# One DVE operation for the bias of the attention's exponentials, in a fused adaLN, attention and mixture-of-experts kernel

## The reference, cut to what matters

```python
ctx_k = jnp.concatenate([sink_k, win_k], axis=2)       # 4 sinks, then a window of 128
logits = jnp.einsum('bhqd,bhkd->bhqk', q, ctx_k) * scale
logits = jnp.where(mask, logits, -jnp.inf)             # cols <= rows + (t_ctx - t)
w = jax.nn.softmax(logits, axis=-1)
w = jnp.where(jnp.isnan(w), jnp.zeros_like(w), w)
out = jnp.einsum('bhqk,bhkd->bhqd', w, ctx_v)
```

## Time and profile before

| | us |
|---|---|
| three runs | 356.20, 357.07, 358.56 |
| median | 357.07 |
| the profiled execution, its own time | 358.24 |
| its span, first to last instruction | 356.5 |
| what lies around the span | 1.74 |
| PE / DVE / ACT / POOL busy in the span | 284.6 / 236.4 / 163.0 / 203.9 |

### The profile page before, as it was taken

How to read it: one execution, slowest core, us unless ns; L and a number is a source line. 1 busy time by engine, 2 the same in 40 slices (tenths; PEclk the granted TensorE clock), 3 DMA queues, 4 the chain that set the end, 5 groups by cost and what they waited for, 6 DMA issues and landing times.

```text
span 356.5 us, 6304 instructions
## 1 busy us (share of the span) xinstructions
PE 284.6 (80%) x1665; PEld 219.3 (62%) x1666; DVE 236.4 (66%) x911; ACT 163.0 (46%) x518; POOL 203.9 (57%) x254
## 2 busy tenths in 40 slices
PE   4898889888989798989865899899979899986000
PEld 4364466656857485747634798789878787775000
DVE  0476477998789887997884654644443577753991
ACT  3142552267135733456212355455544566653550
POOL 3613107728674677558467265556645478773981
PEclk9996996999799996999886699999999999998655
DMA  7949001123615629702285543455546678857895
GB/s 271 310 135 340 3 2 59 62 72 122 192 49 160 178 88 324 182 30 76 75 223 189 199 143 112 149 150 163 157 129 197 190 238 252 259 170 243 305 332 182
DMA packets 41439, 59.81 MB, mean 168 GB/s; under 512 B 5092, under 2 KB 29880, under 8 KB 41404
## 3 DMA queue, kind: packets, MB, share of 16 engines
q1 hardware_dynamic: 34312, 39.91, 38.4%
q0 software_dynamic: 6528, 17.90, 13.9%
q10 hardware_dynamic: 564, 1.59, 1.2%
HBM read 33.57 MB, written 25.80 MB: 167 GB/s over the span
## 4 chain that ended last, share of the span: by engine, by line
PE 40%; DVE 28%; DMA 9%; issue 8%; another core or an unknown queue 5%; ACT 4%; POOL 2%; SPq 1%; DVEq 0%; POOLq 0%; ACTq 0%
PE bank L1225 13%; PE bank L1235 8%; PE bank L890 6%; PE bank L1083 4%; DMA p_win<-slots 3%; PE bank L1050 2%; DVE st L1338 2%; DVE h_sb L1364 2%; PE bank L1027 2%; DVE xs L1386 2%; DMA ht<-in_L_attn_x_dram 2%; PE bank L933 1%; DVE top_i L1381 1%; DVE act_sb L1376 1%
## 5 line engine op out<-in xcount | busy, mean ns | idle before, releaser
L646 POOL DMA_INDIRECT ys<-pt_win,row_i x72 | 71.2, 989 | 56.8 <-ACT pt_win L674 30.3
L1225 PE MATMUL bank<-ht,w_now 128*128 128x128 f32 x576 | 79.7, 283 | 5.4 <-DVE xs L1386 5.4
L593 POOL DMA_INDIRECT slots<-h_sb,slot_i x64 | 63.0, 984 | 32.8 <-DVE slot_i L1435 17.4
L1225 PEld LDWEIGHTS bank<-ht,w_now 128*128 128x128 f32 x576 | 73.4, 199 | 6.2 <-DVE xs L1386 5.6
L1733 DVE TENSOR_TENSOR act_t<-bank,sg 128x128 f32<-128x128 f32 x72 | 20.9, 290 | 52.2 <-ACT sg L841 37.0
L1235 PE MATMUL bank<-w_dn,act_t 128*128 x144 | 45.5, 399 | 6.5 <-DVE act_t L1733 4.9
L674 ACT ACTIVATE ht<-bank 128x256 f32<-128x256 f32 x104 | 39.9, 383 | 22.3 <-PE bank L890 17.6
L674 ACT ACTIVATE pt_win<-bank 128x256 f32<-128x256 f32 (+1 forms) x88 | 37.2, 423 | 23.5 <-PE bank L1235 13.0
L1083 PE MATMUL bank<-w_route,ht 128*128 128x272 f32 x128 | 41.3, 450 | 4.8 <-ACT ht L674 1.7
L890 PE MATMUL bank<-ident,p_win 128*128 128x128 f32 x198 | 36.6, 281 | 5.7 <-DMA p_win<-slots 3.8
L841 ACT ACTIVATE sg<-bank 128x128 f32<-128x128 f32 x72 | 20.1, 279 | 44.4 <-PE bank L1225 20.8
(11 more groups left out here) (260 smaller groups left out, 501.3 us busy)
## 6 DMA issues: line engine op xcount, KB each, us to landing
p_win<-slots SPq DMA_DIRECT2D x67, 129.0 KB
slots<-pads SPq DMA_DIRECT2D x28, 129.0 KB
xs<-in_L_attn_x_dram SPq DMA_DIRECT2D x3, 1024.0 KB
wmod_sb<-ys SPq DMA_DIRECT2D x12, 256.0 KB
w_gu<-ys SPq DMA_DIRECT2D x10, 256.0 KB, 2.9
mod_bc<-mod_rows_out SPq DMA_DIRECT2D x4, 512.0 KB, 5.9
w_dn<-in_L_ffn_w_down_dram SPq DMA_DIRECT2D x1, 2048.0 KB
h_sb<-ys SPq DMA_DIRECT2D x8, 256.0 KB
```

Of the source, the lines that this page charges most:

```text
L593: pool.indirect_dma_start(out=slots, out_offset=bass.IndirectOffsetOnAxis(ap=slot_i[:, k, j:j + 1], axis=0), in_=h_sb[:, j, :], in_offset= ...
L646: pool.indirect_dma_start(out=ys, out_offset=bass.IndirectOffsetOnAxis(ap=row_i[:, col:col + 1], axis=0), in_=y_sb[:, k, :], in_offset=Non ...
L1225: last = mm(bank[2 + k % 2][:, half * P:(half + 1) * P], w_now[:, k % 2, c, half * M:(half + 1) * M], ht[:, k, c, :], start=(c == 0), stop ...
```

## The change

The bias of a group becomes one operation on DVE behind the maximum: less_max = min(-SCALE * m_win, less_sink), where less_sink = -SCALE * m_sink is computed once per batch, right behind m_sink. The tile m_all goes. The sinks' exponent becomes SCALE * logit + less_max in one scalar_tensor_tensor, with the same bias as the window's, so ACT's exponential at L713 has no scale any more. Since that operation now reads less_max, it waits for at_sub of the last group first.

```diff
@@ at_exp (ACT)
-                    act.activation(p_sink[:], p_sink[:], ACT.Exp, scale=SCALE).then_inc(S["at_exp"], 1)
+                    act.activation(p_sink[:], p_sink[:], ACT.Exp).then_inc(S["at_exp"], 1)
@@ DVE
             def at_sink_max(b, at):
                 dve.wait_ge(S["at_log"], b * (HG + 1) + 1)
                 at.done(v.tensor_reduce(m_sink[:], ls, AX.X, ALU.max))
+                at.done(v.tensor_scalar(less_sink[:], m_sink[:], -SCALE, None, ALU.mult))
 
             def at_less_max(b, g, at):
 
                 dve.wait_ge(S["at_log"], b * (HG + 1) + g + 2)
                 hs = slice(4 * g, 4 * g + 4)
                 at.done(v.tensor_reduce(m_win[:, hs], lws[g], AX.X, ALU.max))
-                at.done(v.tensor_tensor(m_all[:, hs], m_win[:, hs], m_sink[:, hs], ALU.max))
-                v.tensor_scalar(less_max[:, hs], m_all[:, hs], -SCALE, None, ALU.mult).then_inc(S["at_sub"], 1)
+                v.scalar_tensor_tensor(less_max[:, hs], m_win[:, hs], -SCALE, less_sink[:, hs], ALU.mult, ALU.min)\
+                    .then_inc(S["at_sub"], 1)
 
             def at_sinks_less_max(b):
-                v.tensor_tensor(p_sink[:], ls, m_all[:].unsqueeze(2).to_broadcast([P, H, SINKS]), ALU.subtract)\
+                wait_apart(dve, S["at_sub"], b * (HG + 1) + HG)
+                v.scalar_tensor_tensor(p_sink[:], ls, SCALE, less_max[:].unsqueeze(2).to_broadcast([P, H, SINKS]),
+                                       ALU.mult, ALU.add)\
                     .then_inc(S["at_sub"], 1)
```

More of the change, by code:

```diff
@@ L175, in bass_adaln_attention_moe @@
         m_win = sb("m_win", [P, H])
-        m_all = sb("m_all", [P, H])
+        less_sink = sb("less_sink", [P, H])
         less_max = sb("less_max", [P, H])
```

## The result

The changed kernel takes 352.01 us (median of 4 runs, 351.41 to 353.70); the kernel before, beside it, 357.01 (4 runs, 356.20 to 358.56). The ratio is 0.9862 with a 95% interval of 0.9814 to 0.9911: 1.4% faster, 4.9 us. I had forecast 356.9 with a range down to 355.3.

What follows compares the result with a forecast made beforehand. The prediction took a chain of waits, PE 40% and DVE 28%, as the bound, with four of 16 groups on it. Its terms, -0.22 + 3 x 0.01 = -0.19 us, put on the median 357.07, gave 356.9 us, range 355.3 to 358.6.

Steps and rivals of the forecast that it cites:

- the price of the edited operations: Attention: removed m_all with its wait -0.22 us in batch 0, -0.19 in others; less_sink +0.20 in batches 1 to 3.
- rival B: Batches 2 and 3: POOL's multiplications hold less_sink, 0.58 for 0.17 us, +1.2 in three batches, 358.1 us; chance 0.1.
- the narrow escape that was forecast: Batch 2: less_sink just escapes POOL's pair of multiplications, which ends at 114.86; less_sink on its own at 114.93.
- the sum: Whole kernel: -0.22 us in batch 0 and +0.01 in each of batches 1 to 3, -0.19 together.
- idle time: DVE: busy time falls by 2 to 3 us of 236.4, and almost all of it becomes idle time.
- my -0.19 us: Whole kernel: the forecast's net change in time, likeliest ends -0.25 and +0.06 us.
- groups 1 to 3 of batches 1 to 3 give nothing: Batches 1 to 3: an earlier less_max there is of no use; group 3's saving runs into DVE's idle 0.71 us.
- rival A: Batches 1 to 3, group 3: less_max escapes POOL's L618, DVE 0.61 us earlier three times, 355.1 us; chance 0.07.
- rival C: Behind the last batch: a 6.01 us stretch ends by its own clock, earlier arrival is waited away, 357.1 us; chance 0.2.

Runs made afterwards that it cites:

- after_pad3: The changed kernel with 3 tiny memsets at the head of DVE's stream, against the kernel before: 356.64 us, ratio 0.9994.
- after_third: The changed kernel run again, without padding, beside the padded ones on one chip, against the kernel before: 353.72 us, ratio 0.9895.
- batches123_only: The change in batches 1 to 3 alone, batch 0 in the old form, against the kernel before: 356.73 us, ratio 1.0002.
- before_same: The kernel before, unedited, run once more as a control against itself: 357.06 us, ratio 1.0005.
- before_pad3: The kernel before with 3 tiny memsets at the head of DVE's stream, against the kernel before: 356.79 us, ratio 1.0017.

## Why the prediction was wrong

**Right: the price of the edited operations.** For batch 0 I had -0.22; all eight profiles with the change in batch 0 and in the others, padded or not, on four chips, have 3.79 or 3.80 from the logits of group 3 to down(0, 3) where the unchanged ones have 3.99 or 4.00, so -0.20, and a doubled m_all gives +0.19. By the rule of the Trainium skill ("VectorE: DVE Perf Modes", section "The DRAIN you can't avoid") that the semaphore costs nothing extra, it could have been 0.07; these profiles decide for the rows. The fused operation takes 0.164 (I took 0.17, ends 0.16 and 0.21), p_sink 0.206 for 0.204, less_sink 0.17 in batches 1 to 3 (0.35 in batch 0, where it is off the chain and costs nothing, as forecast). DVE's busy time fell by 4.3 us and not by 2 to 3: the two groups m_all and less_max had 7.9 us with those that POOL held, and less_max and less_sink have 3.5, with no less_max held. From m_sink to the logits of group 2 nothing changes, 3.37 in both.

**Right: rival B does not happen.** The timeline of batch 2 after the change:

```profile
111.70 1.59 POOL L599 TENSOR_TENSOR scaled<-scaled,mod_bc 128x256 f32<-128x256 f32 x2 [2.51 <-ACT scaled L733]
112.96 0.21 DVE L1307 TENSOR_REDUCE m_sink<-bank 128x16 f32<-128x64 f32 x1
113.21 0.17 DVE L1308 TENSOR_SCALAR less_sink<-m_sink 128x16 f32<-128x16 f32 x1
```

POOL ends at 113.29 and less_sink at 113.38, unheld, 0.09 behind: the narrow escape that was forecast (0.04).

**Wrong, the step that failed: the sum has no term for where DVE's later instructions stand in its stream, and takes what the change removes elsewhere to become "idle time".** The sum priced instructions by their durations and by what waits for them, and took everything behind the edited places as moving along unchanged. But removing instructions also moves all later ones to other places in DVE's stream. In batch 1 this alone is worth 0.69 us (32.01 to 31.32 between after_pad3 and after_third), more than three times what I had summed for the whole change: 0.32 of it the late start, and 0.30 to 0.31 a collision with POOL that it had brought about. Over the whole kernel, with everything equal but the place and the three operations, it is 353.72 against 356.64 us. How the 0.69 becomes 2.9 is not shown: the two profiled executions need the same 121.87 us for all the batches, since after_third gives 0.5 back in batch 2, and differ by 3.3 in the experts' stage, which is less than two traces of the kernel before differ by. Off chip B, three places of the changed kernel have 0.9895, 0.9994 and 0.9906, three of the kernel before 1, 1.0017 and 0.9938. With the old place at batch 1's head the change is worth 0.9994 [0.995, 1.0039], which holds the 0.9995 of my -0.19 us, but is too wide to confirm it.
The Trainium skill ("Runtime: NRT & Kernel Launch", section "Instruction fetch mechanics") says that an engine's instructions are refilled in blocks while it executes, and that the fetch is hidden behind the pace at which instructions are issued. By that rule a place in the stream costs next to nothing. The trace agrees on the blocks (packets of 8,192 and 16,384 bytes on two instruction queues); on the hiding it would disagree only if the gap is the fetch's, which is open.

**Not right as it stood: groups 1 to 3 of batches 1 to 3 give nothing.** The escape of rival A did come. The timeline of batch 1, group 3, which answers to the earlier trace rows:

```profile
84.07 0.16 DVE L1315 SCALAR_TENSOR_TENSOR less_max<-m_win,less_sink 128x4 f32<-128x4 f32 x1
84.11 0.74 POOL L618 TENSOR_TENSOR wsd_gated<-wsd_sb,mod_bc 128x256 f32<-128x256 f32 x1
84.15 0.28 DVE L1374 SCALAR_TENSOR_TENSOR act_sb<-sg,bank 128x128 f32<-128x128 f32 x1
...
84.95 0.67 PE L1103 MATMUL bank<-wsd_gated,act_t 128*128 128x256 f32 x2 [0.88 <-ACT act_t L674]
...
85.65 0.48 DVE L1367 SCALAR_TENSOR_TENSOR h_sb<-scaled,rstd,mod_bc 128x256 f32<-128x256 f32 x1 [0.40 <-issue]
```

less_max starts 0.04 us ahead of POOL's L618 and takes 0.16 instead of 0.58; the longest of all sixteen takes 0.18. PE gets nothing of it up to down(1, 3), as argued: that stretch is 6.74 after and 6.71 before. Behind it there is a difference that I had not considered. From down(1, 3) to the values of batch 1, nine traces with the old form in that batch have 3.30 three times and 3.48 to 3.70 six times; nine with the new form have 3.30 nine times. The late one is ACT's copy of group 3's probabilities: in before it idles 0.54 us,

```profile
89.27 0.60 ACT L674 ACTIVATE pt_win<-bank 128x512 f32<-128x512 f32 x1 [0.54 <-PE bank L890]
```

and in batches123_only 0.16:

```profile
89.22 0.60 ACT L675 ACTIVATE pt_win<-bank 128x512 f32<-128x512 f32 x1 [0.16 <-issue]
```

behind the same instructions of ACT and PE in the same order. What sets it free I do not know. A similar stretch of batch 2 is 3.30 or 3.82 in traces of either kind, of one and the same kernel too, so this may be the same sort of chance. It was not tried further.

**What stays open: how 1.0 to 1.4% come together.** In the pair of chip A the stretches of the batches account for 1.5 us, once 0.2 for the work, 0.7 for the place, and in good part the 0.5 of batch 2, which comes and goes in one and the same kernel. So some 0.9 of the 4.9 us have a shown source. The rest would have to lie in the experts' stage, and no pair of traces can place it there: that stage takes 161.7 and 157.5 us in two traces of the kernel before. A gain was measured only on chips that have waits for "another core or an unknown queue". On chip A, after the change (all waits of the span):

```profile
ACT sg L841 <- remote: 11.0, 6, 2.7
ACT ht L674 <- remote: 5.6, 2, 4.0
DVE xs L1389 <- remote: 4.0, 1, 4.0
```

In sum 20.6 us, against 23.1 before (the 15.8 and 6.1 told of above, and 1.2 of ACT's ht) and 19.0 in before_same, of the kernel before. On chips A, C, D and E each profile has its own number and places of them, most of 1.8 to 2.0 us in the chain. The shift of 0.7 does not carry through reliably either: before_pad3 has it in batch 1 (31.31) and is no faster, 1.0017, its batches taking 123.18 in all against 122.86. So rival C, that an earlier arrival is waited away behind the batches, may have something to it; no run tests it. The 6 us piece of the chain behind the last batch that it rested on the earlier trace rows is no fixed part of the kernel: it stands in before and before_pad3, and not in before_same. Whether the change would keep its gain after any further edit to DVE's stream is doubtful: after_pad3 lost it by three operations. With intervals of 0.4 to 0.6% to each side and a control that was off by 0.5% on chip B, the sizes of single ratios are uncertain, but 0.9862, 0.9891 and 0.9895 for the same kernel in three sets of runs, on two chips at least, are not chance.

## What to carry to other kernels

An edit that adds or removes instructions does two things: it changes the work on the path, which can be summed from rows, and it shifts everything behind it in that engine's stream, which can't be read from the trace of before. Where the sum is well under 1%, the second may be the larger one: here it was 0.7 us in one place, and 0.8% between two lengths of padding, against 0.2 us; so test such an edit with a few idle instructions at the stream's head as well, at two or three lengths, before its gain or loss is put down to what it computes. And take more than one chip: the same change was worth 1.1 to 1.4% in three sets of runs and nothing in a fourth, on another chip. A stage's time from one trace of each kernel needs a second trace of the same kernel beside it before a difference is read from it.

## What the runs showed of the hardware

- A late start of 0.31 to 0.32 us, marked "issue", stands ahead of the h_sb of batch 1 in all five traces in which 172 of the recorded instructions of DVE precede it, with a packet of 8,192 bytes on an instruction queue 0.64 to 0.71 us after its start; in the thirteen with 169, 175, 176, 181 or 184 ahead it is gone.
- POOL's multiplication of two SBUF tiles held DVE's counted_b and less_max, which work in SBUF, when they started within it, until it ended: counted_b took 0.48 to 0.50 instead of 0.18, less_max 0.58 instead of 0.16. m_sink, which reads PSUM, was not held (0.21 at 112.96 in after, within POOL's 111.70 to 113.29). A start 0.04 to 0.09 us earlier than POOL's is enough to go free, so a shift of a tenth of a microsecond is worth three to four tenths.
- One chip ran the kernel before in 344.0 us and three others, and the chip of the result, in 356.7 to 357.2, with the batches' part equal to 1 us. The granted clock of its profiled executions is 0.916 on the one, and 0.898 and 0.895 on A and D. The others have waits of up to 6.4 us that the profile can't put down to any engine or queue of the core, and the one has none; how the difference divides between these waits and the clock is open.
- In the experts' stage the same matmuls kept PE busy for 131.7 us at a granted clock of 0.99, 137.0 at 0.96, 138.4 at 0.95 and 140.6 at 0.94.
